# Attention one: the diagonal mask of the row maximum is added on PE, and a head's 36 score blocks fill nine banks

## The reference, cut to what matters

```
qkv = jnp.einsum('bhce,ef->bhcf', xh, Wqkv) + bqkv
q, k, v = jnp.split(qkv, 3, axis=-1)
att = jnp.einsum('bhqe,bhke->bhqk', q, k) / jnp.sqrt(jnp.float32(he))
mask = jnp.tril(jnp.ones((c, c), dtype=att.dtype), k=-1)
att = jax.nn.softmax(att * mask, axis=-1)
out = jnp.einsum('bhqk,bhke->bhqe', att, v)
```

## Time and profile before

| | us |
|---|---|
| median of 3 runs (3102.18 to 3107.34) | 3106.49 |
| span of the profiled execution | 3102.6 |
| PE busy | 2739.3 (88%) |
| DVE busy | 2505.2 (81%) |
| POOL busy | 1897.6 (61%) |
| ACT busy | 1468.1 (47%) |

### The profile page before, as it was taken

The page is one execution under the profiler, slowest core; times in us unless marked ns, Lnnn a source line. Parts: engine busy times, 40 slices in busy tenths (PEclk is TensorE's granted clock), DMA queues, the critical chain, the costliest instruction groups (busy, mean ns, idle before and its releaser), DMA issues. The chain is left out here.

```text
span 3102.6 us, 64827 instructions
## 1 busy us (share of the span) xinstructions
PE 2739.3 (88%) x14614; PEld 1558.5 (50%) x14614; DVE 2505.2 (81%) x9025; ACT 1468.1 (47%) x3554; POOL 1897.6 (61%) x3733
## 2 busy tenths in 40 slices
PE   3788898898889888889868999999999799999998
PEld 1344344444344444344345666666666466666666
DVE  4577777787777787777556999999999799999998
ACT  1455555565556565556513555555555322222222
POOL 3773444444444444444344777777777588888887
PEclk7788898898898898899868999999999899999999
DMA  2433223223323223323130000000000000000000
GB/s 39 86 73 42 32 30 42 28 34 41 38 24 41 34 28 41 42 25 38 22 132 1 1 1 0 0 0 0 0 0 0 1 9 14 14 14 14 14 15 17
DMA packets 60208, 79.78 MB, mean 26 GB/s; under 512 B 20364, under 2 KB 32408, under 8 KB 59416
## 3 DMA queue, kind: packets, MB, share of 16 engines
q1 hardware_dynamic: 55240, 67.74, 15.5%
q0 software_dynamic: 3072, 8.39, 0.9%
q10 hardware_dynamic: 1744, 2.16, 0.2%
HBM read 18.98 MB, written 8.39 MB: 9 GB/s over the span
## 5 line engine op out<-in xcount | busy, mean ns | idle before, releaser
L455 ACT ACTIVATE probs<-scoresT 128x512 f32<-128x512 f32 (+3 forms) x1536 | 692.7, 491 | 526.8 <-PE scoresT L604 518.6
L546 DVE TENSOR_REDUCE cand<-ring 128x4 f32<-128x512 f32 (+3 forms) x1280 | 592.1, 518 | 83.7 <-PE ring L653 79.8
L376 POOL TENSOR_SCALAR_AFFINE_SELECT probs<-probs 128x128 f32<-128x128 f32 x1024 | 292.6, 295 | 537.9 <-ACT probs L455 532.5
L604 PE MATMUL scoresT<-stage 98*128 98x512 bf16 (+3 forms) x1536 | 518.2, 379 | 68.2 <-ACT probs L455 62.1
L653 PE MATMUL ring<-stage 96*128 96x128 bf16 (+3 forms) x2304 | 403.5, 280 | 42.0 <-DMA stage<-parts 14.3
L653 PEld LDWEIGHTS ring<-stage 96*128 96x128 bf16 x2304 | 175.9, 98 | 328.4 <-DVE cand L546 122.7
L618 PE MATMUL pv<-probs,Vg 128*32 128x512 f32 (+3 forms) x3072 | 329.3, 535 | 4.4 <-POOL probs L376 4.3
L604 PEld LDWEIGHTS scoresT<-stage 98*128 98x128 bf16 x1536 | 146.4, 101 | 274.3 <-ACT probs L455 219.3
L553 DVE CUSTOM_DVE_ANT_0 ring<-ring,lower 128x128 f32<-128x128 f32 x1024 | 260.6, 319 | 18.5 <-PE ring L653 18.5
L1125 ACT ACTIVATE hT<-mmT,w_be,w_g 128x128 f32<-128x128 f32 x512 | 185.4, 468 | 155.4 <-PE mmT L1055 155.4
L1064 PE MATMUL mm<-w_W,x2T 128*128 128x512 f32 x512 | 257.6, 626 | 0.0
(11 more groups left out here) (254 smaller groups left out, 5657.7 us busy)
## 6 DMA issues: line engine op xcount, KB each, us to landing
stage<-parts SPq DMA_DIRECT2D x256, 96.0 KB, 3.1
stage<-parts SPq DMA_DIRECT2D x256, 64.0 KB, 3.3
stage<-parts SPq DMA_DIRECT2D x256, 32.0 KB, 3.0
out<-result SPq DMA_DIRECT2D x64, 128.0 KB, 1.7
stage<-ct SPq DMA_DIRECT2D x128, 4.0 KB
w_W<-in_W SPq DMA_DIRECT2D x4, 512.0 KB
h<-in_WT,tok POOLq DMA_INDIRECT x64
stage<-in_tok_ SPq DMA_DIRECT2D x1, 1024.0 KB, 6.4
```

The lines of the kernel that those rows point to most:

```text
L376: nc.gpsimd.affine_select(out=d, in_=d, compare_op=ALU.is_gt, fill=0.0, base=0, pattern=[[1, P]], channel_multiplier=-1).then_inc(mask_ok, 1)
L455: nc.scalar.activation(probs[:, n % 8, lo:hi], scoresT[u % SCORE_BANKS][:, lo % 512:(hi - 1) % 512 + 1], ACT.Exp, scale=SOFT).then_inc(exp ...
L546: ins = nc.vector.tensor_reduce(c[:, i, j:j + n], src[:, P * at:P * (at + n)].rearrange("p (a b) -> p a b", a=n), AX.X, ALU.max)
L604: nc.tensor.matmul(scoresT[u % SCORE_BANKS][:, lo % 512:(hi - 1) % 512 + 1], Ks[0:ROWS, gi, hh, P * kt:P * kt + P], Qs[0:ROWS, gi, hh, lo: ...
```

## The change

Three things change, all in the event `MX` and in what it reads.

- The nine banks are filled by a new table `MAX_PLAN`. Diagonal blocks now stand beside full ones: five of the nine banks hold one or more. The runs are 14 for a head in place of 18 (10 and 8 single blocks).
- The mask is added and no longer multiplied. `future` holds -2^126 on and above the diagonal and 0 below, four copies side by side, bf16. PE adds it by a matmul with the identity `ident_b` into the same bank: 128 columns for each of four banks with one diagonal block (behind the block), and 512 columns for the bank with four (ahead of the blocks).
- DVE reads every bank with one `tensor_reduce` of 512 columns, nine for a head. `cand` has 9 columns for a query tile; one column is never written in any tile and stays 0.

```
+MAX_PLAN = [
+    ([(7, 0, 4)], None, (slice(7, 8), slice(0, 4))),
+    ([(7, 4, 4)], (3, 1), (slice(7, 8), slice(4, 8))),
...
+    ([(5, 4, 2), (6, 4, 2)], (1, 1), (slice(5, 7), slice(4, 6))),
+    ([(1, 0, 2), (2, 0, 2)], (1, 1), (slice(1, 3), slice(0, 2))),
+    ([(0, 0, 1), (2, 2, 1), (4, 4, 1), (6, 6, 1)], (0, 4), (slice(0, 8, 2), slice(7, 8))),
+]
...
-                                if k < len(FULL_BANKS):
-                                    at = 0
-                                    for i, j, n in FULL_BANKS[k]:
-                                        ins = nc.vector.tensor_reduce(
...
-                                        ins = nc.vector.tensor_tensor_reduce(
-                                            src[:, P * a:P * a + P], src[:, P * a:P * a + P], lower[:], 1.0, 0.0,
-                                            ALU.mult, ALU.max, c[:, i, 7:8])
+                                tiles, cols = MAX_PLAN[k][2]
+                                c = cand[:, hh % 2, tiles, cols]
+                                ins = nc.vector.tensor_reduce(
+                                    c, src[:].rearrange("p (t a b) -> p t a b", t=c.shape[1], b=P), AX.X, ALU.max)
...
+                                if every:
+                                    nc.tensor.matmul(out[:], ident_b[:], future[:].rearrange("p a b -> p (a b)"), start=True, stop=False)
...
+                                    if last:
+                                        ins = nc.tensor.matmul(out[:, P * (at - 1):P * at], ident_b[:], future[:, 0, :], start=False, stop=True)
```

More of the change, by code:

```diff
@@ L30 @@
 ROWS = STACK + 2
-FULL_BANKS = [[(4, 0, 4)], [(7, 0, 4)], [(7, 4, 3), (1, 0, 1)], [(6, 0, 4)],
-              [(6, 4, 2), (2, 0, 2)], [(5, 0, 4)], [(5, 4, 1), (3, 0, 3)]]
-MAX_BANKS = len(FULL_BANKS) + 2
+MAX_PLAN = [
+    ([(7, 0, 4)], None, (slice(7, 8), slice(0, 4))),
+    ([(7, 4, 4)], (3, 1), (slice(7, 8), slice(4, 8))),
+    ([(6, 0, 4)], None, (slice(6, 7), slice(0, 4))),
+    ([(5, 0, 4)], None, (slice(5, 6), slice(0, 4))),
+    ([(4, 0, 4)], None, (slice(4, 5), slice(0, 4))),
+    ([(3, 0, 4)], (3, 1), (slice(3, 4), slice(0, 4))),
+    ([(5, 4, 2), (6, 4, 2)], (1, 1), (slice(5, 7), slice(4, 6))),
+    ([(1, 0, 2), (2, 0, 2)], (1, 1), (slice(1, 3), slice(0, 2))),
+    ([(0, 0, 1), (2, 2, 1), (4, 4, 1), (6, 6, 1)], (0, 4), (slice(0, 8, 2), slice(7, 8))),
+]
+MAX_BANKS = len(MAX_PLAN)
+FUTURE = -2.0 ** 126
 SCORE_BANKS, RING_BANKS = 2, 4
@@ L50 @@
 assert UNITS % SCORE_BANKS == 0
-def wait_each(eng, *waits):
-    for sem, value in waits:
-        eng.wait_ge(sem, value)
 def wait_apart(eng, *waits):
@@ L186, in attention_one @@
         ident, ident_b = shared["ident"], shared["ident_b"]
-        lower = sb("lower", [P, P])
+        future = sb("future", [P, 4, P], BF16)
         upper = sb("upper", [P, P])
@@ L208, in attention_one @@
         probs = sb("probs", [P, 8, S])
-        cand = sb("cand", [P, 2, TPB, 8])
+        cand = sb("cand", [P, 2, TPB, 9])
         count = sb("count", [P, TPB], I32)
@@ L359, in _ @@
                 link(nc.gpsimd.memset(minus_half[:], -0.5))
-                triangle(lower, ALU.is_gt, base=0, pattern=[[-1, P]], channel_multiplier=1)
+                link(nc.gpsimd.memset(future[:], 0.0))
+                link(nc.gpsimd.affine_select(out=future[:], in_=future[:], compare_op=ALU.is_gt, fill=FUTURE, base=0,
+                                             pattern=[[0, 4], [-1, P]], channel_multiplier=1))
                 triangle(upper, ALU.is_ge, base=0, pattern=[[-1, P]], channel_multiplier=1)
@@ L537, in run @@
                             src = ring[e[-1][0] % RING_BANKS]
-                            masked = e[2] == "MX" and e[5] >= len(FULL_BANKS)
-                            (wait_apart if masked else wait_each)(dve, (filled, num(e[-1][0], 0) + 1))
+                            dve.wait_ge(filled, num(e[-1][0], 0) + 1)
                             if e[2] == "MX":
                                 hh, k = e[4:6]
-                                c = cand[:, hh % 2]
-                                if k < len(FULL_BANKS):
-                                    at = 0
-                                    for i, j, n in FULL_BANKS[k]:
-                                        ins = nc.vector.tensor_reduce(
[L547 to L552, removed]
-                                        ins = nc.vector.tensor_tensor_reduce(
-                                            src[:, P * a:P * a + P], src[:, P * a:P * a + P], lower[:], 1.0, 0.0,
-                                            ALU.mult, ALU.max, c[:, i, 7:8])
+                                tiles, cols = MAX_PLAN[k][2]
+                                c = cand[:, hh % 2, tiles, cols]
+                                ins = nc.vector.tensor_reduce(
+                                    c, src[:].rearrange("p (t a b) -> p t a b", t=c.shape[1], b=P), AX.X, ALU.max)
                                 ins.then_inc(read_dve, 1)
@@ L648, in run @@
                                     pe.wait_ge(stack_in[hh], 96 * (g + 1))
-                                blocks = FULL_BANKS[k] if k < len(FULL_BANKS) else [
-                                    (i, i, 1) for i in range(4 * (k - len(FULL_BANKS)), 4 * (k - len(FULL_BANKS)) + 4)]
+                                runs, diagonal, _ = MAX_PLAN[k]
+                                every = diagonal == (0, 4)
+                                if every:
+                                    nc.tensor.matmul(out[:], ident_b[:], future[:].rearrange("p a b -> p (a b)"), start=True, stop=False)
                                 at = 0
-                                for i, j, n in blocks:
+                                for i, j, n in runs:
+                                    last = not every and diagonal == (at + n - 1, 1)
                                     ins = nc.tensor.matmul(out[:, P * at:P * (at + n)], Qs[0:STACK, nxt, hh, P * i:P * i + P],
-                                                           Ks[0:STACK, nxt, hh, P * j:P * (j + n)], start=True, stop=True)
+                                                           Ks[0:STACK, nxt, hh, P * j:P * (j + n)], start=not every,
+                                                           stop=(at + n == 4 if every else not last))
                                     at += n
+                                    if last:
+                                        ins = nc.tensor.matmul(out[:, P * (at - 1):P * at], ident_b[:], future[:, 0, :], start=False, stop=True)
                             elif e[2] == "CT":
```

## The result

The changed kernel takes 3053.02 us (median of 4 runs, 3051.49 to 3056.45) against 3105.26 us (median of 4) of the kernel before; the ratio is 0.9835 with a 95% interval from 0.9821 to 0.9849. 3058 was forecast. The profiled span fell from 3102.6 to 3050.8 us.

What follows compares the result with a forecast made beforehand. PE was taken to lead attention one, waiting for DVE's chains at the windows' ends. A turn: -2.5 us ends, +1.3 masks elsewhere, -1.8 clock; -3.0 counted 15 times and -3 once gave 3058 us, range 3020 to 3103.

Steps and rivals of the forecast that it cites:

- The sum: Whole kernel: -3.0 us a turn, counted 15 times, and -3 us once, -48 us in all, giving 3058 us.
- DVE's nine maxima, no masks: On DVE, nine 512-column maxima a head, 5.4 us for 6.5, save about 1.1 us a head, 8.5 us a turn.
- masks on PE, net of cover: On PE, masks add 3.4 us a turn; ACT's waits cover 0.6, taken between 0 and 1.35.
- The price of a mask itself: On PE, each 128-column mask costs 0.056 us, each 512-column mask 0.21 us, at the full clock.
- The ends: At the windows' ends PE's waits for cf fall from 2.85 to 1.8 (gi 0) and 2.63 to 1.0 us (gi 1).
- DVE is free then: At a window's end, DVE has no other bank left when the last fills, so one maximum of 0.68 us leads to `m`.
- I take half: Low clock behind the windows' ends costs up to 3.6 us a turn; the change takes away half, 1.8 us.
- (D): On PE, weight loads at each mask show and the kernel gets slower, 3144 us; chance 0.15.
- (E): PE comes earlier but waits the time back at ACT or the next cf, no change, 3100 to 3106 us; chance 0.10.
- (B): The windows' ends shorten but the low clock stays behind both waits, -1.2 us a turn, 3085 us; chance 0.20.
- (C): Both low-clock stretches go, -4.8 us a turn, 3031 us, or 3020 with full cover by ACT; chance 0.12.
- The once-only parts: In "init", the maxima of four heads stand alone and gain about 0.8 us a head, -3 us in all.

Runs made afterwards that it cites:

- e11: The change made for head 3 of each four alone, heads 0 to 2 as in the kernel before: 3051.6 us, ratio 0.9834 to before.
- e3: The changed kernel with five idle 512-column matmuls put ahead of PE's wait for cf at each window's end: 3040.7 us.
- e4: The kernel before with nine idle 512-column matmuls put ahead of PE's wait for cf: 3075.2 us.
- e7: The changed kernel without mask matmuls and with five idle matmuls ahead of the wait for cf: 3016.9 us.
- e1: The changed kernel with every mask matmul on PE left out, maxima on DVE as in the change: 3051.1 us.
- e2: The kernel before with the masks added on PE and DVE's work unchanged: 3105.9 us, ratio 1.0006 to before.
- e8: The changed kernel with head 3's transpose and its exponential moved behind the window's last score units and value products: 3005.2 us.

## Why the prediction was right

**What bounds the kernel.** Right: the gain came from the two chains at the windows' ends and from the clock behind them. e11 shows it for the chain, e3 and e4 for the clock.

**The sum.** The turn lost 2.94 us where 3.0 was forecast. That it came so near is luck: all three terms were too large, and their errors (0.6 and 0.8 us of gain too much, 1.3 us of cost too much) cancel. With the clock nearly held (e4, e7, e3: 0.96, 0.96, 0.97) they are:

| term, us a turn | forecast | measured |
|---|---|---|
| DVE's nine maxima, no masks | -4.0 (2.5 + 1.28 + 0.25) | -3.4 (e4 to e7) |
| masks on PE, net of cover | +2.8 (3.4 - 0.6) | +1.5 (e7 to e3) |
| clock | -1.8 | -1.0 (what is left of -2.94) |

The price of a mask itself was right: 0.06 and 0.22 us of start distance for 0.056 and 0.21. Its cover was mis-sized: 1.9 of 3.4 us are hidden, where 0.6 us was taken and the bound was 1.35. About half of the 1.9 shows in PE's waits, when e7 and e3, which differ by the masks alone, are compared, 190 to 1300 us (12.9 and 12.6 turns):

```profile
PE scoresT L601 <- ACT probs L463: 52.0, 158, 1.1
PE ring L664 <- POOL cf L423: 18.7, 25, 0.9
PE ring L654 <- DVE cand L551: 2.6, 13, 0.2
```

```profile
PE scoresT L601 <- ACT probs L463: 44.5, 118, 1.1
PE ring L664 <- POOL cf L423: 14.6, 25, 0.8
```

A turn, the masks fill 0.5 us of waits for ACT, 0.3 of waits for `cf` and 0.2 of waits for a bank, 1.0 us in all. The forecast took its 0.6 from the first alone. Before against changed the waits for ACT hide this (3.3 and 3.5 us a turn), because DVE's faster maxima alone lengthen them, to 3.9 in e1 (48.5 us in 12.6 turns). A difference of the clock within its two digits can hide 0.2 us a turn more. The rest of the cover, some 0.7 us, stays open.

**The ends.** Gi 0 as worked out (1.88 us for 1.8). Gi 1 failed at one step: "DVE is free then". It has two banks still to read, so the wait is 1.55 us for 1.0. That is 0.5 us of the 0.6 by which DVE's term was too large.

**The clock.** "I take half" of 3.6 us. The 3.6 us were too high: e4 removes 13 of the 20 us of low clock in a turn, most of what doesn't stay in every kernel, and gains 2.1. The half was about right: the change took away 8 of these 13 us, worth 1.3 us at the measured 0.16 us each (1.0 in the table, where it is the remainder). What the forecast didn't see is who did it: in e1 (no masks) the waits shrink almost as far and the clock is 0.90. It takes the masks as well: in e2 they alone raise it to 0.93 while the waits are still 2.40 us.

**Rivals.** (D), the weight loads, is refuted by the start distances. (E), the time waited back at ACT, is refuted: 3.5 us a turn for 3.3. (B) and (C) are the outer cases of the clock, and it lay between. Median and span: 3053.0 over 3050.8, 2.2 us, not 3.9.

**The once-only parts.** -3 us for "init" was seen at its end (3.9) and was gone at the end of "first". In its place stood 6 us in the last window, which the forecast had no term of its own for. The Trainium skill (TensorE: Matmul & The Clock Gate, section Back-to-back issue gap) with its 81 ns for a matmul of 128 columns in a stream doesn't hold here: the short masks start 0.06 us ahead of what follows.

## What to carry to other kernels

When work moves from one engine to another, price the receiver's part where it stands: here 3.4 us of matmuls cost 1.5, and the change brought a net gain only for the last head before a wait (e11). Where a short chain over other engines ends in a wait, first look for work that can stand inside the wait: moving one transpose behind the rest of PE's own work in the window brought nearly as much as the whole change (43 us beside 52), and the two added up. And an idle matrix engine costs twice; compare kernels at the same granted clock before a part of a change is called free.

## What the runs showed of the hardware that was not expected

- **Work can pay for itself through the clock.** The kernel before with 3.4 us a turn of added matmuls took the same time (3105.9 and 3103.8 us); its granted clock was 0.93 for 0.89, and its waits were about 1 us a turn shorter. Leaving the same work out of the changed kernel saved 2 us, and 24 us when the clock was held.
- **Idle matmuls ahead of a wait shortened the kernel** by 12 and 29 us. Behind gi 0's end the low clock followed the wait of 2.85 us in all 14 turns of the loop and that of 1.88 us in 13 of 14; with 0.79 us left (e3) it stayed away in 10 of 14, with 0.51 (e8) in all. Behind gi 1's end some low clock followed in every kernel, even with 0.36 us of wait.
- **The low clock cost 0.16 us for each us** in a turn, not 0.5. In the last window, which makes no maxima, it cost twice that (24 us of it before, 7 after, 6.2 us gained). That in a turn much of it falls where PE also waits for ACT is a reading, not shown.
- **A mask added by the identity ran at the rate of its columns**: 128 columns 0.06 us and 512 columns 0.22 us from start to start, with a weight load of 0.1 us ahead of each that didn't show.
